# Three places for the split probabilities, and the tile norm first in every even step of VectorE

## What is computed

```python
img_ctx, txt_ctx = context[:, :257], context[:, 257:]
q = rms_norm(x @ q_w + q_b, nq_s)                  # (B, 56, 16 heads, 128)
k_txt = rms_norm(txt_ctx @ k_w + k_b, nkt_s); v_txt = txt_ctx @ v_w + v_b
out_txt = softmax(q k_txt^T / sqrt(128)) v_txt
out_img = the same with ki_w, vi_w over img_ctx
out = (out_txt + out_img) @ o_w + o_b
```

## Time and profile before

| | us |
|---|---|
| median of 3 runs | 1978.85 (1978.16 to 1980.79) |
| the profiled execution | 1980.14 |
| its span, first to last instruction | 1977.2 |

### The profile page before, as it was taken

The page is one execution under the profiler, slowest core; times in us unless marked ns, Lnnn a source line. Parts: engine busy times, 40 slices in busy tenths (PEclk is TensorE's granted clock), DMA queues, the critical chain, the costliest instruction groups (busy, mean ns, idle before and its releaser), DMA issues. The chain is left out here.

```text
span 1977.2 us, 30967 instructions
## 1 busy us (share of the span) xinstructions
PE 1790.6 (91%) x8863; PEld 1558.3 (79%) x8863; DVE 1323.0 (67%) x2522; ACT 967.7 (49%) x1627; POOL 1097.8 (56%) x955
## 2 busy tenths in 40 slices
PE   7899979999999999999999999999993898699998
PEld 6566668888888888788888888887882787598887
DVE  4444457776776777777767767777772565577776
ACT  3444445555555555555555555555542564244343
POOL 1000367778778787777787787877753331033332
PEclk9999989999999999999999999999997999599999
DMA  3356464456454554554454545545524784133332
GB/s 106 130 191 225 167 177 100 102 107 132 111 115 111 121 117 114 118 127 103 106 133 111 114 112 123 114 114 118 108 78 135 263 272 126 50 110 119 111 113 78
DMA packets 417215, 251.17 MB, mean 127 GB/s; under 512 B 350123, under 2 KB 368683, under 8 KB 415372
## 3 DMA queue, kind: packets, MB, share of 16 engines
q1 hardware_dynamic: 417164, 250.54, 49.4%
HBM read 187.70 MB, written 60.10 MB: 125 GB/s over the span
## 5 line engine op out<-in xcount | busy, mean ns | idle before, releaser
L1292 ACT ACTIVATE p_high<-psum,key_rms 128x448 fp32r<-128x448 f32 x384 | 243.9, 635 | 501.6 <-PE psum L1121 478.3
L1365 DVE TENSOR_TENSOR p_low<-psum,p_high 128x448 fp32r<-128x448 f32 x384 | 238.9, 622 | 280.4 <-ACT psum L1294 280.4
L1119 PE MATMUL psum<-u_high,c_high 128*128 128x448 f32 x832 | 307.8, 370 | 26.0 <-DVE psum L1376 13.1
L1121 PE MATMUL psum<-u_high,c_low 128*128 128x448 f32 x832 | 305.3, 367 | 0.0
L1120 PE MATMUL psum<-u_low,c_high 128*128 128x448 f32 x832 | 304.2, 366 | 0.0
L1119 PE MATMUL psum<-p_high,c_high 128*128 128x448 f32 (+1 forms) x768 | 283.9, 370 | 4.9 <-DVE p_low L1365 4.9
L1120 PE MATMUL psum<-p_low,c_high 128*128 128x448 f32 (+1 forms) x768 | 282.1, 367 | 0.0
L1121 PE MATMUL psum<-p_high,c_low 128*128 128x448 f32 (+1 forms) x768 | 281.9, 367 | 0.0
L1552 POOL TENSOR_TENSOR key_rms<-key_ms,minus_half 128x1 f32<-128x1 f32 x209 | 117.2, 561 | 286.5 <-DVE key_ms L1390 284.2
L1376 DVE COPY psum<-beta_wide 128x448 f32<-128x448 f32 x416 | 260.9, 628 | 21.7 <-issue 5.9
L1558 POOL TENSOR_TENSOR c_low<-stage,c_high 128x512 fp32r<-128x512 f32 x208 | 275.3, 1323 | 0.0
(11 more groups left out here) (240 smaller groups left out, 3798.9 us busy)
## 6 DMA issues: line engine op xcount, KB each, us to landing
stage<-in_ctx SPq DMA_DIRECT2D x210, 256.0 KB, 2.8
averages<-o_raw SPq DMA_DIRECT2D x64, 448.0 KB, 5.2
o_stage<-averages SPq DMA_DIRECT2D x32, 896.0 KB, 5.4
u_raw<-absorbed_queries SPq DMA_DIRECT2D x60, 448.0 KB, 5.4
absorbed_queries<-u_stage SPq DMA_DIRECT2D x14, 1792.0 KB, 6.8
beta_wide<-absorbed_biases SPq DMA_DIRECT2D x32, 448.0 KB, 5.3
recip_wide<-reciprocals SPq DMA_DIRECT2D x32, 448.0 KB, 4.1
p_wide<-probs_by_expert SPq DMA_DIRECT2D x32, 448.0 KB, 3.5
```

The lines of the kernel that those rows point to most:

```text
L1119: nc.tensor.matmul(out, high, rhigh, start=start, stop=False, **kw)
L1121: return nc.tensor.matmul(out, low, rhigh, start=False, stop=stop, **kw)
L1292: nc.scalar.activation(p_high[:, half, :], src, ACT.Exp, scale=key_rms[:, t:t + 1])
L1365: return nc.vector.tensor_tensor(out, a, b, ALU.subtract)
```

## The change

`p_high` and `p_low` get three places instead of two; the place of a unit follows the count of averages. `exponentials(u)` waits for the average that last used its place, three averages back, and no longer for `probs_split`. VectorE's norm stands ahead of `take(step - 1)` in all even steps, where before it did so in step 6 only.

```diff
+P_RING = 3
+def probs_slot(u):
+    return (averaged(u) - 1) % P_RING
-        p_high, p_low = sb("p_high", [P, 2, HALF], F32R), sb("p_low", [P, 2, HALF], F32R)
+        p_high, p_low = sb("p_high", [P, P_RING, HALF], F32R), sb("p_low", [P, P_RING, HALF], F32R)
@@ average
-                                 p_high[0:n, half, :], p_low[0:n, half, :], first, last_tile)
+                                 p_high[0:n, probs_slot(u), :], p_low[0:n, probs_slot(u), :], first, last_tile)
@@ exponentials
-                    used = u - 3 if t == LONE + 1 else u - 1
-                    act.wait_ge(av_done, AVERAGES * it + averaged(u - 2) + CREDIT["av_done"])
-                    act.wait_ge(probs_split, UNITS * it + used + CREDIT["probs_split"])
+                    act.wait_ge(av_done, AVERAGES * it + averaged(u) - P_RING + CREDIT["av_done"])
-                    nc.scalar.activation(p_high[:, half, :], src, ACT.Exp, scale=key_rms[:, t:t + 1])
+                    nc.scalar.activation(p_high[:, probs_slot(u), :], src, ACT.Exp, scale=key_rms[:, t:t + 1])
@@ split_probs
-                    sub(p_low[:, half, :], probs_of(u), p_high[:, half, :].bitcast(F32)).then_inc(probs_split, 1)
+                    k = probs_slot(u)
+                    sub(p_low[:, k, :], probs_of(u), p_high[:, k, :].bitcast(F32)).then_inc(probs_split, 1)
@@ body of VectorE
-                    norms_first = step == 2 * LONE + 2
+                    norms_first = step % 2 == 0
                     if norms_first:
                         norm(*ahead(it, step // 2 + 1))
```

## The result

| | before | after |
|---|---|---|
| median us | 1979.8 (4 runs, 1978.2 to 1982.9) | 1935.6 (4 runs, 1932.5 to 1939.1) |
| the profiled execution | 1980.1 | 1939.1 |
| its span | 1977.2 | 1937.0 |
| one batch of the attention loop | 77.60 | 75.11 |

The ratio after to before is 0.9776 (95% interval 0.9754 to 0.9797). Forecast were 1941.6 us and a batch of 75.2. The profiled execution is 41.0 us shorter; 38.5 were forecast for it, and 15 x (77.60 - 75.11) = 37 of the 41 lie in the batches.

The account below looks back on a forecast made before the run. TensorE sets the pace; its losses fall from 6.84 to 4.5 us a batch. Gains of 5, 31, the first batch's and 1 total 38.5 us: 1980.1 to 1941.6 us, 60%, own range 1930 to 1953, full range 1893 to 1960.

Parts of the forecast that it names:

- C, G and H: Steps 4, 10 and 12: Gram product waits for the copied sum, 0.77 us each; all go, 2.31 us a batch.
- A: Step 0: scores wait for their seed; loss 0.96 us before, 0.62 after, gain 0.34, 15 times.
- B and F: Steps 3 and 9: sums wait for the norm, 0.96 and 1.76 us; both go, the second by 0.1.
- K1: New loss from step 2: second split_sum collides with GpSimd's split_u, so average(2) waits for p_low; 1.0 us.
- K2: New loss from step 8: second image split_sum collides with GpSimd's scale_u, p_low(8) comes late; 1.6 us.
- D: Step 8: scores wait for the seed; loss 0.32 us before, 0.55 after.
- E: average(6) waits for p_low; loss 0.53 us before and after.
- average(7): The average after average(6): would then wait about 0.2 us for its p_low.
- The first: Rival, 25%: collision costs little, the difference slips in ahead of c_low or neither waits; 1896 us, 1910 with one half held.
- The second: Rival, 5%: third place buys nothing, ScalarE late for another reason; waits for the copied sum stay, 1978 us.
- the third: Rival, 6%: part of the gain only, norm(5) or c_twice(4) 0.5 to 1 us later; 1950 to 1958 us.
- The slower one: Rival, 4%: all four split_sums of a batch fall under two GpSimd instructions; 52 us slower, 2032 us.

## Why the prediction was right, point by point

**What bounds the kernel.** Right: TensorE's losses per batch account for the batch's length within 0.01 us.

**The third place.** Right: C, G and H are gone. In step 11 the next group behind the scores, the sums, starts at 665.67 and p_high at 665.95, 0.28 us later and not after the average. The two lines below it, VectorE's waits from 300 to 1400 us, show that the norm waits for the Gram product or for c_twice 133 times in some 190 tiles; the prediction had said nearly every tile:

```profile
665.67 0.36 PE L1190 MATMUL psum<-p_sum_high,ones_r 128*128 128x448 f32 x1
...
665.95 0.64 ACT L1297 ACTIVATE p_high<-psum,key_rms 128x448 fp32r<-128x448 f32 x1 [3.28 <-PE psum L1128]
...
DVE junk L1395 <- PE psum L1135: 145.6, 100, 1.6
...
DVE junk L1395 <- POOL c_twice L1577: 35.9, 33, 1.6
```

**The norm first in the even pitch costs nothing.** Right, and tested: 1886.2 us with it in steps 12 to 22, 1888.0 without it; the intervals of the two ratios overlap, and a batch takes 71.80 and 71.79 us.

**A.** 0.79 measured, 0.62 forecast. The term was short at two places, shown by VectorE and TensorE in step 24: the norm starts 0.33 us after the group behind the Gram product, where I took 0.25, and the seed of take(23) starts 0.75 us after its sum, where take(1) had 0.64.

```profile
627.03 0.37 PE L1126 MATMUL psum<-p_high,c_high 128*128 128x448 f32 x1
...
627.36 0.43 DVE L1395 CUSTOM_DVE_ANT_0 junk<-psum,c_twice 128x257 bf16<-128x257 f32 x1 [1.63 <-PE psum L1135]
...
628.25 0.61 DVE L1426 TENSOR_TENSOR p_sum<-psum,p_sum 128x448 f32<-128x448 f32 x1
...
629.00 0.63 DVE L1381 COPY psum<-beta_wide 128x448 f32<-128x448 f32 x1
...
630.71 0.63 DVE L1381 COPY psum<-beta_wide 128x448 f32<-128x448 f32 x1
```

The gain at A was 0.17 and not 0.34, which over 15 batches is 2.5 us less than forecast. The wait itself is what moving the norm costs in step 24; with the old order there it goes (12 us).

**B and F.** Right, both waits are gone. F's margin of 0.1 us held, barely: key_ms is written at 657.94 and the sums start at 658.06.

**K1 and K2.** Right in place, cause and nearly in size: 0.93 and 1.53 for 1.0 and 1.6. The rows alone left open whether the second instruction of split_sum would also be held; it is, 1.60 us for 0.63. The cause was tested by shortening GpSimd's instructions only. The Trainium skill, "SBUF — State Buffer", section "Who interferes with whom", says that the one that comes second is fully blocked; the trace agrees, the cast ended 0.25 us after GpSimd and not sooner. Its 1.34 us is the sum of the wait and of what was left to do.

**D, E, average(7).** 0.46, 0.54 and 0.11 for 0.55, 0.53 and 0.2.

**The sum.** 38.5 us forecast, 41.0 in the profiled execution, 44 between the medians. The forecast's own sum holds a slip: 15 x 2.0 is 30 and not 31, so its terms give 37.5. The losses of a batch were forecast at 4.5 and measured at 4.36, and in part the errors cancel: A was 0.17 too low, D, average(7), K1 and K2 together 0.32 too high. From the first scores to the last sums the loop is 41.4 us shorter, 37 of them in the batches; its ends gave 4 us where I had 2.5. Outside the loop the profiled execution was 0.4 us longer. The rest, 3 us, is the difference between the profiled execution and the median of its kernel, which the four runs (1932.5 to 1939.1) do not settle.

**Rivals.** The first (a cheap collision) falls with the cast's 1.34 and the difference's 1.60 us. The second (a useless third place) falls with the run of the third place alone. Of the third (F or D larger) nothing is seen: F has no wait and D is 0.46. The slower one needed all four split_sums under two GpSimd instructions: that of step 1 met c_twice alone (cast 0.82 us), that of step 7 nothing (cast 0.38 us).

**What the prediction did not say.** It added the parts up for the change as a whole and never asked what each is worth by itself, though its own terms nearly say it: the order wins B and F, 2.72 us a batch, and loses K1, K2 and average(7), 2.8. The third place alone is worth 40 us of the 44, and in the profiled executions all of it. The order on top takes away 3.3 us a batch (the key_ms waits of 0.95 and 1.76 and 0.6 of the seed's wait in step 8) and puts back 3.4 (A 0.79, K1 0.93, K2 1.53, average(7) 0.11). Only with the second split_sum out of the way do both count: 1886.2 us, 94 us under the kernel before, is the best version of these.

| | split_sum in steps 2 and 8 | in steps 3 and 9 |
|---|---|---|
| two places, old order | 1979.8 | not run |
| three places, old order | 1939.0 | 1970.7 |
| two places, norm first | 1955.0 | 1938.9 |
| three places, norm first | 1935.6 | 1898.5 |
| three places, norm first but in step 24 | not run | 1886.2 |

## What to carry to other kernels

When an instruction of an in-order engine is moved ahead, look at what it releases on another engine and at what is then still to come on its own: here the norm released GpSimd 2 us before two SBUF-only instructions of VectorE, and these had slipped in ahead of it before. Work the losses of the bounding engine out wait by wait over one period, with the start-to-start distance, before and after; the sum of them forecast the period to 0.1 us. And try each part alone: two edits that remove different waits of one engine can be worth together what one of them is worth.

## What the runs showed of the hardware

A cast of 448 columns from SBUF to SBUF takes 0.39 us alone, 0.85 begun 0.14 us inside a GpSimd instruction of 0.74 us, and 1.34 begun 1.04 us inside one of 2.13. Whichever begins second is held, GpSimd too (c_low 1.46 us for 1.29), and in these rows the two take turns: between two back-to-back instructions of GpSimd one of VectorE gets through, and the one that depends on it waits for the next gap (K1, K2). A difference with one source in PSUM is not held: p_low at 644.90 takes 0.61 us while GpSimd's c_twice runs from 644.58 to 645.57. Not expected was that shortening VectorE's chain ahead of such an instruction can gain nothing, since it then waits for the same end of GpSimd's (0.74 to 1.27 us, p_low at the same distance).
